# Spreading a value difference over its head's rows: full-height matmuls one by one, or 32-row matmuls in pairs

## What is computed

```python
vq = x @ vq_w.T
v, q = jnp.split(vq, 2, axis=-1)
k = jax.nn.sigmoid(x @ key_w.T + key_b)
upd = (1.0 - k)[..., :, None] * v[..., None, :]
decay = k[..., :, None]
...
_, kv = jax.lax.associative_scan(combine, (decay, upd), axis=1)
h = jnp.einsum('nthd,nthde->nthe', qh, kv).reshape(n, t, HID)
return h @ out_w.T + out_b
...
idx = jnp.argmax(jax.nn.log_softmax(logits) + gumbel)
out = jnp.einsum('btd,de->bte', x, W[idx]) + b[idx]
```

## Time and profile before

| what | value |
|---|---|
| median of 3 runs | 222.52 us (221.82 to 222.86) |
| profiled execution: its own time | 223.1 us |
| span of the profiled execution | 221.2 us |
| PE, DVE, ACT, POOL busy | 192.3, 153.9, 112.7, 79.4 us |
| mean granted TensorE clock | 0.969 of full |

### The profile page before, as it was taken

The page is one execution under the profiler, slowest core; times in us unless marked ns, Lnnn a source line. Parts: engine busy times, 40 slices in busy tenths (PEclk is TensorE's granted clock), DMA queues, the critical chain, the costliest instruction groups (busy, mean ns, idle before and its releaser), DMA issues.

```text
span 221.2 us, 3102 instructions
## 1 busy us (share of the span) xinstructions
PE 192.3 (87%) x972; PEld 145.2 (66%) x972; DVE 153.9 (70%) x385; ACT 112.7 (51%) x172; POOL 79.4 (36%) x67
## 2 busy tenths in 40 slices
PE   6659886978996999999999999999997989999940
PEld 6128664466873767788877868897774767666820
DVE  0378957897978679978868899777896227671143
ACT  2497923123027764322298732225996346895630
POOL 4020006121011902751345739233469332354401
PEclk9997998899999999999999999999999999999985
DMA  5995020100000010000000100000001000001001
GB/s 132 316 431 216 15 59 1 47 0 0 3 0 0 0 52 1 0 0 3 0 0 1 47 0 0 0 0 0 0 3 49 0 0 0 0 3 47 0 3 50
DMA packets 6125, 8.19 MB, mean 37 GB/s; under 512 B 480, under 2 KB 4832, under 8 KB 5728
## 3 DMA queue, kind: packets, MB, share of 16 engines
q1 hardware_dynamic: 6112, 8.02, 10.7%
HBM read 6.97 MB, written 1.05 MB: 36 GB/s over the span
## 4 chain that ended last, share of the span: by engine, by line
issue 34%; PE 23%; POOL 19%; DVE 11%; ACT 5%; DMA 4%; SPq 1%; POOLq 1%; DVEq 0%
PE c_bank L803 10%; POOL rstd L292 5%; POOL hid_even_low L308 5%; POOL hid_odd_low L308 4%; DMA xt<-x_tok 4%; POOL res L287 4%; PE y_bank L771 3%; PE b_bank L790 3%; DVE state L564 3%; DVE normed_lent L549 2%; PE b_bank L936 2%; DVE read L572 1%; ACT hid L415 1%; DVE stats L532 1%; PE b_bank L785 1%
## 5 line engine op out<-in xcount | busy, mean ns | idle before, releaser
L292 POOL TENSOR_TENSOR rstd<-varied,power 128x4 f32<-128x4 f32 x16 | 17.8, 1114 | 78.4 <-DVE varied L542 78.4
L564 DVE TENSOR_TENSOR_SCAN state<-rep_bank,keep 128x256 f32<-128x256 f32 x64 | 39.8, 670 | 4.6 <-PE rep_bank L763 4.5
L771 PEld LDWEIGHTS y_bank<-attend_pack,read 128*128 128x128 f32 x256 | 33.0, 198 | 13.2 <-DVE read L572 11.5
L771 PE MATMUL y_bank<-attend_pack,read 128*128 128x128 f32 x256 | 36.0, 287 | 5.4 <-DVE read L572 4.8
L308 POOL TENSOR_TENSOR hid_even_low<-hid,hid_even_high 128x512 fp32r<-128x512 f32 x16 | 20.4, 1283 | 34.4 <-ACT hid L415 24.8
L413 ACT ACTIVATE hid_even_high<-c_bank,scales_pack 128x512 fp32r<-128x512 f32 x16 | 11.0, 689 | 27.7 <-PE c_bank L803 27.7
L415 ACT ACTIVATE hid<-c_bank,scales_pack 128x512 f32<-128x512 f32 x32 | 21.8, 682 | 0.0
L572 DVE TENSOR_TENSOR read<-state,query 128x512 f32<-128x512 f32 x32 | 21.4, 679 | 0.0
L803 PE MATMUL c_bank<-hid_even_high,hidden_rounded 128*128 128x512 f32 x64 | 19.7, 414 | 0.6 <-ACT gate L390 0.6
L803 PE MATMUL c_bank<-hid_even_low,hidden_rounded 128*128 128x512 f32 x64 | 18.9, 400 | 0.4 <-DVE hid_even_low L595 0.4
L803 PE MATMUL c_bank<-hid_odd_high,hidden_rounded 128*128 128x512 f32 x64 | 19.2, 412 | 0.0
(11 more groups left out here) (129 smaller groups left out, 359.8 us busy)
## 6 DMA issues: line engine op xcount, KB each, us to landing
hidden_pack<-hidden SPq DMA_DIRECT2D x2, 1024.0 KB, 11.8
attend_pack<-attend SPq DMA_DIRECT2D x1, 1152.0 KB, 7.7
xT_lent<-x_chan SPq DMA_DIRECT2D x4, 256.0 KB, 8.6
xt<-x_tok SPq DMA_DIRECT2D x4, 256.0 KB, 3.2
mlp_pack<-mlp SPq DMA_DIRECT2D x1, 768.0 KB, 9.6
out<-xT_lent SPq DMA_DIRECT2D x3, 256.0 KB, 2.3
metric_pack<-metric SPq DMA_DIRECT2D x1, 384.0 KB, 13.2
project_pack<-project SPq DMA_DIRECT2D x1, 256.5 KB, 2.7
```

The costliest lines, as they stand in the source:

```text
L292: nc.gpsimd.tensor_tensor(rstd[n][:], varied[n][:], power[:], ALU.pow).then_inc(ln_rstd[n], 1)
L564: ins = nc.vector.tensor_tensor_scan(state[:, e % STATES, at], rep_bank[e % 2][:, at], keep[:, bass.ds(a * T + s * SEQ, SEQ)], 0.0, ALU.ad ...
L771: ins = nc.tensor.matmul(y1_bank[:, tile(j)], read[:, e % READS, tile(j)], out_w_rep_sb[:, e, :], start=(e == 0 and j == 0), stop=False, s ...
```

## The change

- The value channels are ordered by their number in the head and not by head, and in strips: the 16 values with number e of all heads stand in rows of strip e % 4 of the 128 partitions, together with those of e + 4. The weights that make or read values are permuted on the host.
- `replicate_pair(a, e)` replaces two calls of `replicate`. It gives four matmuls, each on the 32 rows of one strip: rounded part of e, rounded part of e + 1, rest of e, rest of e + 1. It waits for the scans of both e-2 and e-1.
- Each `replicate_pair` stands where the first of its two calls stood, and DVE's list is put in pairs as well: two scans, two reads. Between norm_out and the scan pair 4 and 5 there now stand scan 3 and reads 2 and 3.
- The 0/1 matrices come as a small table in a new pack "heads" (128 KB), and ACT spreads it into `rep_r` ahead of the first projections. The attend pack shrinks to 640 KB. The mask `blocks` moves to the metric pack.
- The rounded part of the difference is cast by ACT (`high_values`), for groups 1 to 3 in the step before; `low_values` on DVE stands ahead of `norm_out(0, a)`.
- The three projections of group 1 move from the end of step 0 to the middle: on PE behind pair 0 and pair 2, on ACT ahead of the routing.

```diff
 PACKS = (
-    ("project", (("key_w", P), ("value_w", P), ("query_w", P), ("blocks", P), ("key_b", 1))),
-    ("attend", (("rep", HD * P), ("out_b", P), ("out_w_rep", HD * P), ("out_w", P))),
...
+    ("project", (("key_w", P), ("value_w", P), ("query_w", P), ("key_b", 1))),
+    ("heads", (("rows_of", HD * HEADS), ("head_sum", P))),
+    ("attend", (("out_b", P), ("out_w_rep", HD * P), ("out_w", P))),
...
+        def strip(e):
+            return slice(e % 4 * P // 4, (e % 4 + 1) * P // 4)
...
                 sp.dma_start(xT[:, at], x_chan[:, at]).then_inc(xT_loaded[g], 16)
                 if g == 0:
+                    load_pack("heads")
                     load_pack("scales")
                     load_pack("attend")
...
                     ins.then_inc(proj_out, 1)
-                    if n == 1:
-                        act.wait_ge(loaded["attend"], 16)
-                        nc.scalar.copy(rep_r[:], rep_sb).then_inc(rep_cast, 1)
+            def high_values(a):
+                act.wait_ge(dv_whole, nth(a, 1, 1))
+                if not first(a):
+                    act.wait_ge(rep_ready, nth(a, RP, 0))
+                nc.scalar.copy(dvalue_parts[0][:], dvalue[:]).then_inc(dv_high, 1)
...
                     nc.scalar.activation(spare[:], ones[:, 0:1], ACT.Sigmoid)
+                    act.wait_ge(loaded["heads"], 16)
+                    nc.scalar.copy(rep_r[:].rearrange("p e (h d) -> p e h d", h=HEADS),
+                                   rows_of_sb.unsqueeze(3).to_broadcast([P, HD, HEADS, HD])).then_inc(rep_cast, 1)
...
                     projections(range(0, PROJECTIONS))
+                    high_values(a)
+                    projections(range(PROJECTIONS, 2 * PROJECTIONS))
                     act.wait_ge(loaded["scales"], 16)
                     routing()
                     round_weights()
                     for i in range(len(MLP_PACKS)):
                         sum_low_halves(i)
-                    projections(range(PROJECTIONS, 2 * PROJECTIONS))
+                    high_values(a + 1)
...
-                    nc.vector.tensor_copy(dvalue_parts[0][:], dvalue[:]).then_inc(dv_high, 1)
...
-                    if c is not None:
-                        read_state(a, 1)
+                    read_state(a, 1)
+                    if first(a):
+                        route_on(0)
                     scan(a, 2)
                     if first(a):
-                        route_on(0)
-                    if c is None:
-                        read_state(a, 1)
-                    if first(a):
                         route_on(1)
                 if b is not None:
                     norm_out(1, b)
...
-                if first(b):
-                    dve.wait_ge(proj_out, 3 * PROJECTIONS - 1)
-                    value_steps(a + 1)
...
                 if a is not None:
                     for e in range(6, HD):
                         scan(a, e)
-                        read_state(a, e - 1)
-                    read_state(a, HD - 1)
-                if a is not None and c is not None:
+                    for e in range(6, HD):
+                        read_state(a, e)
+                if a is not None:
+                    if first(a):
+                        dve.wait_ge(proj_out, 2 * PROJECTIONS - 1)
+                    if first(b):
+                        dve.wait_ge(proj_out, 3 * PROJECTIONS - 1)
                     value_steps(a + 1)
...
                 if a is not None:
+                    low_values(a + 1)
                     norm_out(0, a)
...
-            def replicate(a, e):
+            def replicate_pair(a, e):
                 if e == 0:
                     pe.wait_ge(dv_ready, nth(a, 1, 1))
                 if not first(a) or e >= 2:
-                    pe.wait_ge(scan_done, nth(a, RP, e - 1))
...
+                    pe.wait_ge(scan_done, nth(a, RP, e))
+                for i in range(2):
+                    for n in (e, e + 1):
+                        ins = nc.tensor.matmul(rep_bank[n % 2][:], rep_r[strip(n), n, :], dvalue_parts[i][strip(n), :],
+                                               start=(i == 0), stop=(i == 1))
+                        if i == 1:
+                            ins.then_inc(rep_ready, 1)
...
                 if a is not None:
-                    replicate(a, 2)
+                    replicate_pair(a, 2)
+                    if first(a):
+                        project(PROJECTIONS + 2)
+                        pe.wait_ge(loaded["attend"], 16)
                     attend(a, c, 0)
-                    replicate(a, 3)
                     attend(a, c, 1)
                 if b is not None:
...
                     transposes(b, 1)
                 if a is not None:
-                    replicate(a, 4)
+                    replicate_pair(a, 4)
                     attend(a, c, 2)
```

77 lines of the change are left out of this document (39 added, 38 removed).

## The result

| | median | runs | against before |
|---|---|---|---|
| before | 222.69 us | 4 (221.82 to 223.12) | |
| after | 229.34 us | 4 (228.81 to 229.88) | 1.0304, 95% interval 1.0264 to 1.0344 |

The change makes the kernel slower by 3.0%, some 6.7 us. The forecast was 225.2 us: the side is right, and the time lies outside the range. The profiled execution has a span of 228.0 us (before 221.2) and a mean granted clock of 0.941 (0.969).

The account below looks back on a forecast made before the run. PE looked like the bound of the loop steps, DVE of step 0. Step 0 +2.4, step 1 -0.5, its end +0.6, steps 2 and 3 +0.2: +2.7 on a median of 222.52 gives 225.2 us, range 221.3 to 227.6.

Parts of the forecast that it names:

- The routing wait: Step 0: DVE's first route instruction waits 4.7 us for ACT's routing behind group 1's projection copies; last read +3.8 after scan 1.
- The start: Start of step 0: heads land at 6.2, first scan at 11.85 instead of 13.23, a gain of 1.4 us (0.6 to 2.3).
- Moving the three projections away from the end of step 0 gives nothing: End of step 0: group 1's projections lay beside the norm, so moving them changes the time by nothing.
- Step 1 and its end: Step 1: norm_sum(2, 0) at 60.8 before 61.53, -0.5 us; its end: low_values ahead of norm_out(0, 1), +0.6 us.
- Steps 2 and 3: Loop steps: -0.45 us to hidden(2, 2), +0.4 for low_values, +0.15 for contention; +0.1 each (-0.4 to +1.3).
- The walk: Steps 2 and 3: sum of PE's work behind scan 3, 16.45 us, with hidden(2, 2) at 105.95 instead of 106.40.
- The wait for scan 3: Steps 2 and 3: pair 4 on PE waits for scan 3, PE idle about 1 us.
- that turn: Steps 2 and 3: reads 2 and 3 in a row beside POOL's subtractions slow DVE, +0.15 us (0 to +0.5).
- The pair itself: PE time of one replicate pair: strips overlap, with one emptying of the array, 0.65 us (bounds 0.47 and 1.25).
- The faster one: Rival: PE is the bound, waits are covered, pairs cost 0.47 in steps 1 to 3; 219.4 us, chance 0.12.
- The second: Rival: heads at 5.3 gives 0.9 us more and loop steps the bare -0.45 each; 223.2 us, chance 0.20.
- The third: Rival: strips don't overlap, 1.25 us a pair, six pairs lie bare, +3.6 us; 228.8 us, chance 0.13.

Follow-up runs that it names:

- g3: f4 with group 1's three projections moved forward on PE and ACT as in the change, routing behind them, one replicate at a time at full height: 224.53 us, 1.0129.
- h3: f4 with group 1's projections moved forward and ACT's routing chain ahead of them: 221.48 us, 0.9968.
- h1: f4's kernel unchanged, measured once more: 220.09 us, 0.9838.
- f4: Kernel before with only the early 0/1 matrices (small heads pack, early ACT cast), full height: 220.45 us, 0.9893.
- e1: Kernel after with ACT's routing ahead of group 1's three projections instead of behind them: 226.4 us, 1.0111.
- h2: f4 with 32-row strip matmuls, one replicate at a time, nothing else changed: 229.84 us, 1.0302.
- e2: Kernel after with group 1's three projections back at the end of step 0 on PE and ACT, its value differences behind norm_out: 226.83 us, 1.0175.
- g2: f4 with the pair order and the pairs' matmuls in 32-row strips: 222.13 us, 1.0001.

## Why the prediction was wrong in size

- **The routing wait: right.** 4.7 forecast, 4.79 measured; step 0 +2.4 and +2.46. That the two agree so closely is some luck: the first scan came 0.28 earlier than forecast (11.57 for 11.85), and the way from it to the last read took about 0.3 longer. Between g3 and h3, which differ in the order of ACT alone, the wait is worth 1.6 points of ratio, 3.6 us.
- **The start: too small.** The heads landed at about 5.3, the lower end (h1 4.8, f4 5.9), and the first scan came 1.66 earlier, not 1.4. Where nothing takes it back (f4) `total` comes 3.1 earlier: the idle 0.97 of the earlier trace rows goes too, because in f4 the clock does not fall in those scans.
- **"Moving the three projections away from the end of step 0 gives nothing": this step failed.** They cost PE nothing there and kept it at work. Without them it idles 4.33 us, and the clock is at half from 37.1 to 43.9. Of the +1.43 at the border 0.36 is the norm, the other 1.07 the slow PE behind it. e1 has the same +1.43 with the routing wait removed, and the eight profiles against nine show the longer stretch with no exception. The Trainium skill, "TensorE: Matmul & The Clock Gate", Part 1, says that the gate goes by how busy PE has been; this row agrees, while h2, at half clock for 20 us with PE's records busy throughout, does not.
- **Step 1 and its end: right.** -0.88 for -0.5, and +1.08 for +0.6. Of the former 0.41 is a slow start of the kernel before, whose replicate 0 takes 0.98 us at the end of its second stretch (40.05 to 41.03; 0.57 in f4). Of the latter 0.4 is the clock: e1, whose profile has no fall there, shows 13.68 us for 14.07.
- **Steps 2 and 3, "+0.1 each": this step failed too.** The walk, which counts strips and pair order together, put `hidden(2, 2)` 0.45 earlier; it came 0.09 later. The wait for scan 3 was right (about 1 us forecast, 0.85). But `norm_out(1, b)`, which I took to stay where it was, comes 0.09 later behind replicate 0 (7.89 for 7.80). And most prices of the walk behind it were a few hundredths low: 16.45 in the walk, 16.81 in the trace (93.77 to 110.58), just as long as before (89.59 to 106.40). Reads 2 and 3 do take 2.50 us where two take 1.27, beside POOL's subtractions, but PE waits for none of it, so the +0.15 for that turn is not seen on its path. Held against f4 the pair order costs 0.52 and its strips give back 0.33, +0.19 and not -0.3; the low part costs 0.36, within what I gave it (+0.4). The pair itself was right: 0.65 taken, 0.66 measured.
- **The clock was in no term.** In the earlier trace rows it is 1.00 and I carried that over. The last stretch from step 3 on takes 92.23 with a fall and 90.58 in e2, whose loop step has the same length and no fall: 1.65 us. With the one behind step 0 and the one at the end of step 1, some 3.1 of the 4.1 us by which the forecast was short of 6.8 are the half clock; most of the rest is the loop steps (0.44 and 0.4). This goes by one profile of each kernel.
- **Rivals.** The faster one (PE the bound) took 0.47 for a pair, which measured 0.66, and fell since PE is not the only bound: it idled 0.63 us in the step before, 1.58 after. The second (the stall is given back) had its condition met, heads at 5.3, but that gave 0.3 us more and not 0.9, and the loop steps gave nothing. The third (pairs one by one, 228.8) came nearest in time by another cause.

What stays open is why a fall comes at 71 or at 140 in one kernel and at 92 or 170 in another, and in one profile of a kernel and not in the next (f4, h1). PE's gaps of about 1 us are near them, but the same gaps pass without a fall in step 2. The parts' ratios, put one on another (-1.1, +0.6, +0.5, +2.4, +1.6 points), give +4.0 for 3.0 measured. Each ratio has an interval of 0.4 to 0.6, which makes some 1.4 for the sum, so the runs do not tell whether the parts add up. For the same reason the +0.6 and +0.5 of the pair order and of its strips are not clear of nothing one by one; in the loop step they are, in one profile each.

## What to carry to other kernels

A step moved out of an engine's idle time costs or gains nothing by its duration alone: look at what it moves past on every queue it passes (here ACT's routing behind three copies) and at what is left in the hole on TensorE, since TensorE came back at half clock, for 6.8 us or more, from every hole of 4 us at this place. Put an edit of several parts on the chip one part at a time: here one part gave 1.1 to 1.6%, the other four, put on it one by one (the strips on the pair order), cost 5 points of ratio in sum. And reduce TensorE's work only where it is TensorE that ends the wait.

## What the runs showed of the hardware

- Two 32-row fp32r matmuls of 512 columns in different strips overlap: a pair of replicates, four matmuls, takes 0.66 us with strips and 0.93 without. Two matmuls in the same strip show no overlap: one replicate alone takes 0.65 where it takes 0.47 at full height (127.93 to 128.40 in the kernel before). This row is of h2:

```profile
91.17 0.50 PE L769 MATMUL rep_bank<-dvalue_high,rep_r 32*128 32x512 f32 x1
91.50 0.38 PE L770 MATMUL rep_bank<-dvalue_low,rep_r 32*128 32x512 f32 x1
91.82 1.16 PE L778 MATMUL y_bank<-attend_pack,read 128*128 128x128 f32 x8
```

  So here 32-row matmuls one by one are dearer than full ones, by 0.18 a replicate. The Trainium skill, "TensorEngine Tiling (Array Packing)", Key Properties, has a drain at a change of mode; by it the excess would be that drain, and these rows agree in direction.
- TensorE stayed at half clock for some 20 us (h2, 15.1 to 35.5) while its records are busy 21.77 of 22.00 us, when replicates of 32 rows stood between full-height attends. At full height, at the same place, it rose after 3.4 us (h1). With 32-row matmuls in pairs (g2) it rose after 3.4 us too. What makes the difference is open.
- A 128x512 read on DVE with two SBUF inputs took 1.25 us beside POOL's subtraction (two in 2.50 at 94.87 of the kernel after; 0.67 alone), and POOL's root of 128x4 took 1.40 for 1.03 beside such an instruction (36.41 after, 33.96 before).
